# Attention stage: a half's sixteen units in batches of five, five and six, maxima 27 units ahead

## The reference, cut to what matters

```
q = (x @ q_w.T).reshape(b, s, 16, 32).transpose(0, 2, 1, 3)   # 16 heads of 32
k = x @ k_w.T                                                  # one head of keys
v = x @ v_w.T                                                  # one head of values
scores = einsum('bhqd,bkd->bhqk', q, k) / sqrt(32)
attn   = softmax(scores, axis=-1)
out    = einsum('bhqk,bkd->bhqd', attn, v)                     # 2 x 16 x 2048 x 2048 probabilities
```

## Time and profile before

| | |
|---|---|
| median of 3 runs | 4882.86 us (4879.08 to 4890.41) |
| the profiled execution's own time | 4881.05 us |
| its span | 4879.5 us |
| the attention stage's batches | from about 989 us to 2545 us of the span |
| PE busy over the span | 4676.6 us (96%) |
| maximum reduces, L1465 DVE | 2048, 1251.6 us busy, 680 ns each |
| exponentials, L1417 ACT | 2048, 1039.7 us busy, 620 ns each |
| additions of pairs, L1452 POOL | 512, 1257.6 us busy, 2474 ns each |

### The profile page before, as it was taken

The page is one execution under the profiler, slowest core; times in us unless marked ns, Lnnn a source line. Parts: engine busy times, 40 slices in busy tenths (PEclk is TensorE's granted clock), DMA queues, the critical chain, the costliest instruction groups (busy, mean ns, idle before and its releaser), DMA issues. The chain is left out here.

```text
span 4879.5 us, 89290 instructions
## 1 busy us (share of the span) xinstructions
PE 4676.6 (96%) x30668; PEld 3646.1 (75%) x30669; DVE 2928.3 (60%) x5643; ACT 2241.4 (46%) x4559; POOL 2327.1 (48%) x1772
## 2 busy tenths in 40 slices
PE   6999996999999999999998799999999999999999
PEld 4788885666666666666656588887899987689998
DVE  6222225789999999999965522222655558674444
ACT  4222224466666666666662322222544435453433
POOL 1545434178888888888870335451411016420000
PEclk8999997899999999999999899999999999999999
DMA  7223226657777777777766523332532221251110
GB/s 220 79 92 101 91 83 223 245 109 147 147 147 147 147 147 147 147 147 147 147 125 192 181 84 99 94 99 65 193 99 92 88 90 59 69 192 51 53 53 32
DMA packets 253579, 593.91 MB, mean 122 GB/s; under 512 B 31680, under 2 KB 85952, under 8 KB 228800
## 3 DMA queue, kind: packets, MB, share of 16 engines
q0 software_dynamic: 62224, 317.75, 28.9%
q1 hardware_dynamic: 191024, 271.73, 16.9%
HBM read 262.74 MB, written 121.63 MB: 79 GB/s over the span
## 5 line engine op out<-in xcount | busy, mean ns | idle before, releaser
L1452 POOL TENSOR_TENSOR attend_pairs<-attend_pt 128x1024 f32<-128x1024 f32 x512 | 1257.6, 2474 | 196.3 <-ACT attend_pt L1417 196.1
L1465 DVE TENSOR_REDUCE attend_mx<-attend_am_ps 128x1 f32<-128x512 f32 x2048 | 1251.6, 680 | 123.8 <-PE attend_am_ps L1325 120.5
L1417 ACT ACTIVATE attend_pt<-attend_sc_ps 128x512 f32<-128x512 f32 x2048 | 1039.7, 620 | 283.4 <-PE attend_sc_ps L1313 283.3
L1325 PE MATMUL attend_am_ps<-attention_kst,attend_qst 96*128 96x512 f32 x2048 | 859.2, 425 | 8.9 <-DMA attend_qst<-q_parts 8.7
L1313 PE MATMUL attend_sc_ps<-attend_qst,attention_kst 98*128 98x512 f32 x2048 | 816.3, 400 | 1.5 <-ACT attend_pt L1417 1.3
L1325 PEld LDWEIGHTS attend_am_ps<-attention_kst,attend_qst 96*128 96x128 f32 x2048 | 393.4, 192 | 239.2 <-DVE attend_mx L1465 123.3
L718 DVE TENSOR_TENSOR expert_ac<-expert_gu_ps,expert_gl 128x512 f32<-128x512 f32 x144 | 99.6, 692 | 670.7 <-ACT expert_gl L682 670.6
L1339 PE MATMUL attend_pv_ps<-attend_pt,attention_v 128*32 128x256 f32 x8192 | 493.6, 381 | 0.0
L1313 PEld LDWEIGHTS attend_sc_ps<-attend_qst,attention_kst 98*128 98x128 f32 x2048 | 389.8, 191 | 87.3 <-ACT attend_pt L1417 11.7
L1339 PEld LDWEIGHTS attend_pv_ps<-attend_pt,attention_v 128*32 128x32 f32 x8192 | 246.2, 110 | 211.5 <-ACT attend_pt L1417 46.2
L1820 ACT ACTIVATE ffn_sg<-ffn_gu_ps,ffn_gs 128x256 f32<-128x256 f32 x352 | 166.7, 474 | 508.2 <-PE ffn_gu_ps L1741 508.2
(11 more groups left out here) (347 smaller groups left out, 9126.4 us busy)
## 6 DMA issues: line engine op xcount, KB each, us to landing
attend_pairs<-attend_pairs POOLq DMA_DIRECT2D x189, 1024.0 KB, 7.4
weights_raw<-experts_dram POOLq DMA_DIRECT2D x76, 512.0 KB, 4.2
ys<-expert_ob SPq DMA_DIRECT2D x144, 256.0 KB, 2.3
attend_qst<-q_parts SPq DMA_DIRECT2D x192, 128.0 KB, 3.9
yn<-route_yb SPq DMA_DIRECT2D x64, 256.0 KB, 3.7
ffn_xb<-x SPq DMA_DIRECT2D x64, 256.0 KB, 2.8
ffn_rb<-x SPq DMA_DIRECT2D x64, 256.0 KB, 3.0
keyvalue_xb<-x SPq DMA_DIRECT2D x64, 256.0 KB, 2.8
```

Of the source, the lines that this page charges most:

```text
L1325: pe.matmul(am[:, bank, :], qst[0:KROWS, n % 2, h * HALF + hd, :], kst[0:KROWS, o:o + 4 * P], start=True, stop=True).then_inc(am_rdy, 1)
L1417: act.activation(pt[:, u % RING, g * 4 * P:(g + 1) * 4 * P], sc[:, s % SBANKS, :], ACT.Exp, scale=HD ** -0.5).then_inc(p_rdy, 1)
L1452: pool.tensor_tensor(pairs[:, slot(half, j), :], pt[:, 2 * p % RING, :], pt[:, (2 * p + 1) % RING, :], ALU.add).then_inc(pair_rdy, 1)
L1465: dve.tensor_reduce(mx[:, hh, block:block + 1], am[:, am_slot["max", a] % MBANKS, :], AX.X, ALU.max).then_inc(mx_rdy, 1)
```

## The change: three batches for a half instead of four

The sizes are 5, 5 and 6 units, the maxima run 27 units ahead instead of 28 (so that a half's last maximum still closes its first batch), and `turn` is placed by counting maxima: still behind the fourth of a half, which is the fourth of the second batch. The reciprocals move: two pieces after the second batch's maxima, one after the third's, one with the product after the next first batch's, where `lowest` is too. ACT's two copies stay where they were by meaning: behind a half's last values, and behind the values of a half's first batch. The number of matmuls, reduces, exponentials, additions and DMAs is the same.

```
-BATCH = 4
+SIZES = (5, 5, 6)
-LEAD = 28
+LEAD = 27
-SHARES_AT = ((0,), (1, 2), (3,), ())
+SHARES_AT = ((0, 1), (2,), (3,))
+TURN_AFTER = 4
...
+        def batch(c):
+            half, at = divmod(c, PER_HALF)
+            return half * QT + sum(SIZES[:at]), SIZES[at]
+
+        def turn_due(a):
+            half, at = divmod(a - TURN_AFTER + 1, HPIECES)
+            return half - 1 if at == 0 and 0 < half <= HALVES else None
...
+            for a in range(2 * LEAD):
+                highest(a)
+            for s in range(SBANKS):
+                score(s)
+            for c in range(BATCHES):
+                first, n = batch(c)
+                for i in range(2 * n):
+                    highest(2 * (first + LEAD) + i)
+                    if 2 * first + SBANKS + i < PIECES_ALL:
+                        score(2 * first + SBANKS + i)
                 half, at = divmod(c, PER_HALF)
...
-                for u in range(c * BATCH, (c + 1) * BATCH):
+                for u in range(first, first + n):
                     values(u)
...
-                act.wait_ge(pv_rdy, RING + min(QT * (half + 2) + BATCH, N * UNITS))
+                act.wait_ge(pv_rdy, RING + min(QT * (half + 2) + SIZES[0], N * UNITS))
...
+            def highest(a):
+                if a < PIECES_ALL:
+                    maxi(a)
+                    if (a + 1) % HPIECES == 0:
+                        lowest(a // HPIECES)
+                if turn_due(a) is not None:
+                    keep(turn_due(a))
...
                     for piece in SHARES_AT[at]:
                         shares(half, piece)
-                    if at == 2:
+                    if at == PER_HALF - 1:
                         output(half)
```

More of the change, by code:

```diff
@@ L1236, in attention_stage @@
         HALVES = 2 * N
-        BATCHES = N * UNITS // BATCH
+        PER_HALF = len(SIZES)
+        BATCHES = HALVES * PER_HALF
         PIECES_ALL = 2 * N * UNITS
         HPIECES = 2 * QT
[L1240 to L1246, removed]
-        am_use = []
[L1249 to L1254, removed]
+        def batch(c):
[4 more added lines that the diff above has]
+            return half - 1 if at == 0 and 0 < half <= HALVES else None
+        am_use = []
+        for a in range(PIECES_ALL + TURN_AFTER):
+            if a < PIECES_ALL:
+                am_use.append(("max", a))
+            if turn_due(a) is not None:
+                am_use.append(("turn", turn_due(a)))
         am_slot = {use: k for k, use in enumerate(am_use)}
@@ L1355, in sums @@
                     add_up(half, j, False, j == 1)
[L1357 to L1370, removed]
+            def highest(a):
+                if a < PIECES_ALL:
+                    maxi(a)
+                if turn_due(a) is not None:
+                    turn(turn_due(a))
+            for a in range(2 * LEAD):
[8 more added lines that the diff above has]
+                        score(2 * first + SBANKS + i)
                 half, at = divmod(c, PER_HALF)
@@ L1417, in _ @@
                 act.activation(pt[:, u % RING, g * 4 * P:(g + 1) * 4 * P], sc[:, s % SBANKS, :], ACT.Exp, scale=HD ** -0.5).then_inc(p_rdy, 1)
[L1418 to L1422, removed]
+                half, at = divmod(s + 1 - SBANKS, HPIECES)
+                if at == 0 and half >= 1:
+                    keep_values(half - 1)
+                if at == 2 * SIZES[0] and half >= 2:
                     keep_sums(half - 2)
@@ L1512, in _ @@
                         shares(half, piece)
-                    if at == 2:
+                    if at == PER_HALF - 1:
                         output(half)
-            for half in range(HALVES - 2, HALVES):
-                for piece in range(PIECES):
+            for half in range(HALVES - 3, HALVES):
+                for piece in SHARES_AT[-1] if half == HALVES - 3 else range(PIECES):
                     shares(half, piece)
```

## The result

| | us |
|---|---|
| changed kernel, median of 5 runs | 4912.19 (4911.27 to 4914.76) |
| kernel before, median of 5 runs | 4885.16 (4879.08 to 4890.41) |
| ratio | 1.0059, 95% interval 1.0048 to 1.0070 |
| span of the profiled execution | 4913.2 against 4879.5 |

The direction was as forecast. The size was 27 us between the medians where 20 was forecast, and 4912.19 lies 0.19 over the top of the range. It is 11.4 us over the forecast's 4881.05 + 19.7: 4.1 because the kernel before measured 4885.16 here, and 7.3 because the change cost 27.0 and not 19.7.

A forecast was written before the change was run, and what follows sets the result against it. PE was taken to bound the attention stage, DVE close behind. Per half, 0.66 us of added stalls less the 0.33 saved switch; 62 x 0.33 = 20.5, -1.2, +0.4, on 4881.05 gives 4901 us; range 4873 to 4912.

The forecast's parts named there:

- What bounds the stage: Attention stage: PE, busy all the time, sets the end; DVE at 92% falls behind 0.129 us with every maximum inside a batch.
- The saved switch, 0.33: PE, going from whole-array to quarter matmuls and back: one of four changes in a half removed, saving 0.33 us.
- Rival B: PE's array-mode switch costs 0.77 us, more than forecast; half 0.11 us shorter, 4873 us; chance 0.12.
- The stalls 0.06, 0.58, 0.32: PE's waits for DVE to free one of the maxima's four banks, in us, in the first, second and third batch.
- Rival A: The maxima's four banks absorb the longer runs; half 24.04 us, total 4860 us; chance 0.08.
- Is DVE free at each start? ... a reciprocal and the product 1.1: DVE between batches: done at 7.9 us in the first, before the next first maximum at 8.10 + 0.55; no delay.
- Rival D: DVE starts the third batch late, overrunning its 0.25 us spare by 0.2; 12 us more, 4913 us; chance 0.08.
- ACT and POOL at nothing: ACT's exponentials and POOL's pair additions keep up with the longer batches; cost zero, bounded by 0.3 us a half.
- The maxima's DMAs, no cost: Two DMAs from `keep` to the next half's first score: cover 8.8 us, issue 1.33, landing 3.9; no wait.
- The ends and the sum: Fewer maxima before the first score, -1.2 us; last two halves, +0.4; 62 halves at 0.33 more, 20.5 us.

## Why the prediction missed its range, step by step

- **What bounds the stage.** Right. PE sets the end and DVE's lag inside a batch is what PE waits for. (The prediction's "16th" score is the batch's 16th matmul, its eighth score; the step of 0.2343 is read rightly.)
- **The saved switch, 0.33.** Right in size: 0.36 with DVE made fast. Rival B's 0.77 is out. What in a batch's own cost is the switch stays open.
- **The stalls 0.06, 0.58, 0.32.** Right: batches of 8.10, 7.74 (with the product moved) and 8.86, and 9.37 for a size that no trace had shown. Rival A is out: the banks don't absorb ten or twelve maxima.
- **"Is DVE free at each start? ... a reciprocal and the product 1.1".** This step failed. The product was priced at a row in which POOL's addition happened to end 0.33 us after it began. In the first batch of five POOL still has 1.3 us to go, the product takes 1.56, and DVE is free at 8.80 instead of 7.9, against 8.65 needed. So the second batch took 7.89 and not 7.75. That is 0.15 a half, 24.85 instead of 24.70; over 62 halves 9.3 us, beside the 7.3 by which the medians miss. The prediction took its check of spare time to be tightest in the second batch, by 0.25; it was short in the first, where it saw 0.75. Moving the product took 6.3 us off the median, cutting POOL's additions took 11 off in one run. Without it the change would have measured near 4903 to 4906, inside the range (an estimate, from 4912.19 less 9.3 and from the run with the product moved). Rival D had the mechanism in general form (DVE late at a start), but in the third batch, where the first reduce began on time, 0.54 behind the start (2248.84 against 2248.30). That its 4913 us lies within 1 us of the measured time is luck. The rows that showed the product's wait stood in the prediction's own groups: 2209.11 on POOL, 2209.40 on DVE.
- **ACT and POOL at nothing.** Right for ACT: first exponentials follow their scores by 0.43 as before. For POOL right as a supplier, wrong as a neighbour.
- **The maxima's DMAs, no cost.** Right: the cover was 8.8, the last landing in the changed kernel came 4.0 to 5.6 us behind `keep` where 5.2 was taken, and the smallest margin was 3.2. The price rested on the landings of other DMAs, though, and it was luck that it fitted: with the turn later in the batch the same two took 7.3 to 8.6.
- **The ends and the sum.** From its first weight load of a maximum (956.1 and 956.9) to ACT's last copy (2551.2 and 2582.8) the stage grew by 30.8 us in the traces; 19.7 + 9.3 explain 29.0. The rest up to the span's 33.7 lies in other stages and was not looked into; the medians differ by 27.

## What to carry to other kernels

When a fast engine feeds a slower one through n banks in bursts, the burst's length has a limit: here the reducer falls behind by 0.129 us with each maximum, and by the sum four banks with a release of 0.74 us carry nine of them before PE waits. Lengthening a burst to save a fixed cost pays only up to there, and anything that takes a place in the ring counts, the transpose too; put it where the ring is idle. Before a DVE operation with two SBUF inputs is priced from a row, look at what POOL ran beside it: the row's duration may be a wait.

## What was not expected of the hardware

- A product of 128x256 in SBUF took 0.42 us with POOL idle, and 0.62, 0.97 or 1.56 by how long POOL's running addition still had to go; all 112 of the kernels before and after ended 0.27 to 0.30 behind such an addition's end. Where another addition followed with no gap, 12 of 59 waited for that one too and took 3.0 us.
- Two DMAs of 4 KB from SBUF to SBUF were ready 2.5 to 3.2 us after their data with no DMA of the pairs beside them, and 4.0 to 8.6 with one of 1 MB, by where it lay (1.3 of it the issue of both). A wait of about 2 us on PE for them was followed by the lower clock in 40 of 44 halves; wait and clock cost 4.3 us a half in the mean (28.92 against 8.10 + 7.70 + 8.85).
- A batch has a cost of its own of 0.33 to 0.36 us, with one change from whole-array to quarter matmuls and back in it, and a `turn` costs 0.08 to 0.12.
